# Routing and experts of a two-layer decoder as one block: shared tiles, 40 plain indirect transfers, places mapped expert by expert

## The reference

```python
x = x_btd.reshape(N, Dm)                       # 2048 tokens, already normalised
cap = int(math.ceil(CF * N / E))               # 308 places for each of 8 experts
probs = jax.nn.softmax(x @ Wr + br, axis=-1)
gates, ids = jax.lax.top_k(probs, K)           # K = 2
order = jnp.lexsort((-flat_g, flat_ids))       # by expert, highest gate first
rank = jnp.arange(M) - starts[s_ids]
valid = rank < cap                             # only the 308 highest of an expert are kept
xg = x[disp_tok].reshape(E, cap, Dm)
h = jax.nn.silu(jnp.einsum('ecd,edh->ech', xg, W1) + b1[:, None, :])
out = jnp.einsum('ech,ehd->ecd', h, W2) + b2[:, None, :]
gated = out * disp_g.reshape(E, cap, 1)
y = jnp.zeros((N, Dm), x.dtype).at[disp_tok].add(gated.reshape(E * cap, Dm))
```

## Time and profile before

| | us |
|---|---|
| median of 3 runs | 600.41 (596.93 to 601.2) |
| the profiled execution | 599.32 |
| its span, first to last instruction | 597.2 |
| TensorE busy, share of the span | 469.0, 79% |
| VectorE busy | 332.1, 56% |
| ScalarE busy | 240.4, 40% |
| GpSimd busy | 209.2, 35% |

### The profile page before, as it was taken

The page is one execution under the profiler, slowest core; times in us unless marked ns, Lnnn a source line. Parts: engine busy times, 40 slices in busy tenths (PEclk is TensorE's granted clock), DMA queues, the critical chain, the costliest instruction groups (busy, mean ns, idle before and its releaser), DMA issues. The chain is left out here.

```text
span 597.2 us, 13480 instructions
## 1 busy us (share of the span) xinstructions
PE 469.0 (79%) x5103; PEld 374.5 (63%) x5103; DVE 332.1 (56%) x917; ACT 240.4 (40%) x514; POOL 209.2 (35%) x234
## 2 busy tenths in 40 slices
PE   3899999999986978999999988992663332499950
PEld 1587777777763757899988877781553221266630
DVE  5567677777753535666666652637755667011114
ACT  3766666666552326555555522230220000132313
POOL 3556687799133214000000010316430000557750
PEclk9899999999996999999999987997575555599995
DMA  7970312200000002000000003000024000333317
GB/s 234 386 292 6 143 61 61 63 3 2 4 1 1 0 7 76 1 0 0 0 0 0 0 2 88 19 1 0 1 77 134 1 0 0 103 96 106 113 33 211
DMA packets 31461, 34.72 MB, mean 58 GB/s; under 512 B 5562, under 2 KB 25079, under 8 KB 31289
## 3 DMA queue, kind: packets, MB, share of 16 engines
q1 hardware_dynamic: 29208, 29.50, 15.6%
q0 software_dynamic: 2064, 4.60, 2.4%
q10 hardware_dynamic: 144, 0.00, 0.0%
HBM read 28.65 MB, written 5.46 MB: 57 GB/s over the span
## 5 line engine op out<-in xcount | busy, mean ns | idle before, releaser
L473 DVE TENSOR_REDUCE at_nmax<-bank 128x4 bf16<-128x512 f32 x128 | 82.5, 686 | 44.0 <-PE bank L569 44.0
L413 ACT ACTIVATE at_p<-bank 128x512 f32<-128x512 f32 x128 | 69.2, 596 | 38.2 <-PE bank L588 38.2
L95 POOL TENSOR_TENSOR var<-var,eps 128x12 f32<-128x12 f32 (+1 forms) x8 | 1.6, 206 | 176.4 <-DVE var L88 176.4
L1902 POOL DMA_INDIRECT mo_rows<-mo_n_rows,mo_src_row x24 | 23.0, 959 | 71.3 <-POOLq L1610 64.3
L582 PE MATMUL bank<-ident_b,at_nmax 128*128 128x128 bf16 x512 | 42.8, 221 | 4.3 <-DVE at_nmax L473 3.4
L582 PEld LDWEIGHTS bank<-ident_b,at_nmax 128*128 128x128 bf16 x512 | 30.7, 98 | 18.9 <-issue 9.3
L1975 ACT ACTIVATE mo_h<-bank,mo_b 128x308 f32<-128x308 f32 x32 | 16.5, 517 | 47.5 <-PE bank L1938 47.5
L608 PE MATMUL bank<-at_p,at_v 128*32 128x128 f32 x1024 | 34.7, 276 | 0.9 <-DVE x L490 0.9
L1946 PE MATMUL bank<-mo_w,mo_h 128*128 128x128 f32 (+1 forms) x192 | 33.0, 294 | 1.3 <-ACT mo_h L1975 1.3
L1946 PEld LDWEIGHTS bank<-mo_w,mo_h 128*128 128x128 f32 (+1 forms) x192 | 24.3, 173 | 12.1 <-ACT mo_h L1975 5.3
L1081 PE MATMUL bank<-li_v,li_am 128*128 128x65 f32 x256 | 30.4, 272 | 0.5 <-issue 0.5
(11 more groups left out here) (280 smaller groups left out, 1193.1 us busy)
## 6 DMA issues: line engine op xcount, KB each, us to landing
fo_w<-in_up_stages SPq DMA_DIRECT2D x9, 512.0 KB, 9.3
fo_w<-in_down_stages SPq DMA_DIRECT2D x9, 512.0 KB, 4.7
at_k_ctx<-in_ctx_heads SPq DMA_DIRECT2D x1, 4096.0 KB, 23.9
mo_w<-in_L_ffn_W SPq DMA_DIRECT2D x16, 256.0 KB, 3.1
mo_planes<-ro_zeros POOLq DMA_DIRECT2D x1, 2048.0 KB, 9.1
mo_got<-mo_planes SPq DMA_DIRECT2D x8, 256.0 KB, 5.1
x<-in_x SPq DMA_DIRECT2D x4, 256.0 KB, 3.6
au_ctx<-in_ctx SPq DMA_DIRECT2D x4, 256.0 KB, 3.4
```

The lines of the kernel that those rows point to most:

```text
L413: act.activation(m.p[:, s % 2, J * g:J * g + J, :], bank_t[g][:, :].rearrange("p (j t) -> p j t", j=J), ACT.Exp, scale=scale).then_inc(exp ...
L473: dve.tensor_reduce(m.nmax[:, J * g:J * g + J], bank_s[g % 2][:, :].rearrange("p (j t) -> p j t", j=J), AX.X, ALU.max, negate=True).then_i ...
L1902: pool.indirect_dma_start(out=rows[0:m, e % 2, r, :], out_offset=None, in_=n_rows, in_offset=bass.IndirectOffsetOnAxis(ap=src_row[0:m, til ...
```

## The change

The two blocks become one, `experts` (L1543 of the new kernel), so that engines pass from routing to experts without a common end. Its parts:

- The normalised tokens of all groups stay in one buffer `n` of 136 columns per sequence, 128 features and the 8 values `v`. They are stored as one table after the softmax, rows of 544 bytes, so that a gathered row brings its gates along.
- The softmax and the two highest take 18 operations, some of them interleaved. GpSimd computes which plane an entry goes to (`kind`) while the search begins.
- The search is written out for 10 rounds, with pieces of 6, 6 and 4 sequences.
- Two experts share 5 tiles: two full ones each and one in the middle that holds 52 rows of one expert from row 0 and 52 of the other from row 64. That makes 20 gathers and 20 scatters. Every row of a tile is fetched and stored; unused ones go to spare rows of the planes, so no bounds check is needed.
- Places are mapped expert by expert: `mark` (two comparisons of 1024 columns) and `index` on VectorE, `mapping` (16 matmuls with 6 columns, and one more for the second expert of a pair) on TensorE. Three maps stand before the first transpose, the other five in the loop, each between the second `up` and the first `down`.
- ScalarE copies the transposed rows (`copy_x`) and multiplies the output bias by the gates (`bias`); VectorE's `gate` multiplies the expert's output by the gates and adds that. At the end only two additions per group remain.
- Planes are read back in 4 loads of 512 KB, two from SyncE's and two from ScalarE's queue, and the result is stored from both. Clearing the planes moves from GpSimd's to SyncE's queue. The weights of the first two experts are loaded during the routing.
- The loops over experts are written out.

The core of the diff (indentation shortened):

```diff
-ROWS = [min(128, CAP - r) for r in range(0, CAP, 128)]
-TILES = E6 * len(ROWS)
...
+REST = CAP - 256
+TILES = 5
+SHARED = 2
+ROW = D + E6
+KINDS = 2 + E6
+PIECES = (slice(0, 6), slice(6, 12), slice(12, B))
+FIRST_GATHERS = 2 * TILES
+LATER_GATHERS = (3, 2, 3, 2, 0, 0, 0, 0)
...
-with pe.Fori(0, BITS // ROUND) as i:
-    for b in range(B):
-        if b % HALF == 0:
-            pe.wait_ge(reached_done, 2 * i + b // HALF + 1)
-        mm = pe.matmul(bank_c[:, 0:TRIALS * E6], ones_b[:, :],
-                       reached[:, b, :, :].rearrange("t j e -> t (j e)"),
-                       start=(b == 0), stop=(b == B - 1))
-    mm.then_inc(compared, 1)
...
-for half in range(2):
-    seqs = slice(HALF * half, HALF * half + HALF)
-    dve.tensor_tensor(reached[:, seqs, :, :],
...
-with dve.Fori(0, BITS // ROUND // UNROLL) as i:
-    for k in range(UNROLL):
-        search(UNROLL * i + k)
...
-done(dve.tensor_tensor(at, over(lanes[:, 0:TILES], 2 * B),
-                       hi[:, :, :].rearrange("t k b -> t (k b)").unsqueeze(2)
-                       .to_broadcast([T, 2 * B, TILES]), ALU.is_equal))
...
-dve.wait_ge(lanes_made, 1)
-for k in range(2):
-    dve.tensor_tensor(at_row[:, k, :, :], over(lanes_b[:, :], B),
-                      lo[:, k, :].unsqueeze(2).to_broadcast([T, B, 128]), ALU.is_equal)\
-        .then_inc(rows_marked, 1)
-dve.wait_ge(mapped, 1)
-code, token = code_sum[:, 1, :], code_sum[:, 0, :]
-done(dve.tensor_copy(code_sum[:, :, :], bank_m[:, 0:2 * TILES].rearrange("p (c s) -> p c s", c=2)))
...
-done(dve.tensor_scalar(src_row[:, :], dst_row[:, :], B * T - 1, None, ALU.bitwise_and))
...
-gather(0)
-gather(1)
-for e in range(E6):
-    if e + 2 < E6:
-        pool.wait_ge(turned, e + 1)
-        gather(e + 2)
-    pool.wait_ge(y_added, e + 1)
-    scatter(e)
...
-up(e, par, 0)
-up(e, par, 1)
-down(e, par, 0, first)
-up(e, par, 2)
-down(e, par, 1)
-up(e, par, 3)
-down(e, par, 2)
-if not last:
-    turn(e + 1, 1 - par)
-down(e, par, 3)
...
-for g in range(groups):
-    act.wait_ge(fetched[g], 32)
-    for b in range(Q * g, Q * g + Q):
-        act.activation(got[:, 0, b, :], got[:, 0, b, :], ACT.Copy, scale=gate[0][:, b:b + 1])\
-            .then_inc(gated, 1)
...
-for g in range(groups):
-    dve.wait_ge(fetched[g], 32)
-    for b in range(Q * g, Q * g + Q):
-        dve.scalar_tensor_tensor(out=core.x[:, b, :], in0=got[:, 1, b, :], scalar=gate[1][:, b:b + 1],
-                                 in1=core.x[:, b, :], op0=ALU.mult, op1=ALU.add).then_inc(x_part, 1)
-    seqs = slice(Q * g, Q * g + Q)
-    dve.wait_ge(x_part, Q * (g + 1))
-    dve.wait_ge(gated, Q * (g + 1))
-    dve.tensor_tensor(core.x[:, seqs, :], core.x[:, seqs, :], got[:, 0, seqs, :], ALU.add)\
-        .then_inc(x_done, 1)
...
+def places(e):
+    if e % 2 == 0:
+        return ((0, slice(0, 128), slice(0, 128)), (1, slice(0, 128), slice(128, 256)),
+                (SHARED, slice(0, REST), slice(256, CAP)))
+    return ((SHARED, slice(64, 64 + REST), slice(0, REST)), (3, slice(0, 128), slice(64, 192)),
+            (4, slice(0, 128), slice(192, 320)))
...
+def fetch(eng, g):
+    seqs = slice(Q * g, Q * g + Q)
+    eng.dma_start(got[:, :, seqs, :], by_token[:, 0:2, seqs, :]).then_inc(fetched[g], 16)
...
+sp.wait_ge(levelled, 1)
+sp.dma_start(table[0:B * T, :].rearrange("(t b) c -> t b c", t=T), n[:, :, :]).then_inc(t_out, 16)
+sp.dma_start(table[B * T:B * T + B, :], n[0:B, 0, :]).then_inc(t_out, 16)
...
+def gather(first, last):
+    for at in range(first, last):
+        pair, tile = divmod(at, TILES)
+        pool.wait_ge(indexed, 4 * pair + (3 if tile >= SHARED else 1))
+        pool.indirect_dma_start(
+            out=rows[:, pair, tile, :], out_offset=None, in_=table,
+            in_offset=bass.IndirectOffsetOnAxis(ap=src_row[:, pair, tile:tile + 1], axis=0))\
+            .then_inc(x_in[2 * pair + (tile > SHARED)], 16)
+def scatter(pair, tile):
+    pool.wait_ge(y_done, 6 * pair + (1, 2, 4, 5, 6)[tile])
+    pool.wait_ge(indexed, 4 * pair + (4 if tile >= SHARED else 2))
+    pool.indirect_dma_start(
+        out=planes,
+        out_offset=bass.IndirectOffsetOnAxis(ap=dst_row[:, pair, tile:tile + 1], axis=0),
+        in_=y[:, pair, tile, :], in_offset=None).then_inc(stored, 16)
...
+pool.wait_ge(levelled, 1)
+pool.tensor_tensor(kind[0][:, :], flat(pick[0]), kinds[:, 128:256], ALU.mult).then_inc(kind_step, 1)
...
+gather(0, FIRST_GATHERS)
+at = FIRST_GATHERS
+for e in range(E6):
+    for tile in (range(0, SHARED) if e % 2 == 0 else range(SHARED, TILES)):
+        scatter(e // 2, tile)
+    gather(at, at + LATER_GATHERS[e])
+    at += LATER_GATHERS[e]
...
+    first, count = (0, 3) if e % 2 == 0 else (3, 2)
+    act.activation(xT[:, e // 2 % 2, first * 128:(first + count) * 128], bank_x[:, 0:count * 128],
+                   ACT.Copy).then_inc(x_copied, 1)
+def bias(e):
+    act.wait_ge(x_in[e], 48 if e % 2 == 0 else 32)
+    if e >= 2:
+        act.wait_ge(y_done, 3 * (e - 1))
+    for r, (tile, at, _) in enumerate(places(e)):
+        ins = act.activation(gb2[at, e % 2, r, :], b2[at, e, :], ACT.Copy,
+                             scale=rows[at, e // 2, tile, D + e:D + e + 1])
+    ins.then_inc(biased, 1)
...
+for i in range(ROUNDS):
+    for k, seqs in enumerate(PIECES):
+        pe.wait_ge(reached_done, len(PIECES) * i + k + 1)
+        for b in range(seqs.start, seqs.stop):
+            mm = pe.matmul(bank_c[:, 0:TRIALS * E6], ones_b[:, :],
+                           reached[:, b, :, :].rearrange("t j e -> t (j e)"),
+                           start=(b == 0), stop=(b == B - 1))
+    mm.then_inc(compared, 1)
...
+def mapping(e):
+    pair, odd = divmod(e, 2)
+if odd:
+    pe.wait_ge(indexed, 4 * pair + 2)
+elif pair >= 2:
+    pe.wait_ge(indexed, 4 * (pair - 1))
+for k in range(2):
+    pe.wait_ge(marked, 2 * e + k + 1)
+    for b in range(B // 2 * k, B // 2 * k + B // 2):
+        mm = pe.matmul(bank[:, 4 * odd:4 * odd + 6], at_row[:, e % 2, b, :],
+                       codes[:, :, :, b, e].rearrange("t k c -> t (k c)"),
+                       start=(not odd and b == 0), stop=(b == B - 1), skip_group_check=True)
+if odd:
+    mm = pe.matmul(bank[:, 2 * SHARED:2 * SHARED + 2], core.ident_b[:, :],
+                   spare_b[:, 2 * pair:2 * pair + 2],
+                   start=False, stop=True, skip_group_check=True)
+mm.then_inc(mapped, 1)
...
+for e in range(3):
+    mapping(e)
+turn_x(0)
+for e in range(E6):
+    up(e, 0)
+    up(e, 1)
+    if e + 3 < E6:
+        mapping(e + 3)
+    down(e, 0)
+    up(e, 2)
+    down(e, 1)
+    up(e, 3)
+    down(e, 2)
+    if e + 1 < E6:
+        turn_x(e + 1)
+    down(e, 3)
...
+for seqs in PIECES:
+    count = seqs.stop - seqs.start
+    dve.tensor_tensor(reached[:, seqs, :, :],
...
+def mark(e):
+    if e >= 2:
+        dve.wait_ge(mapped, e - 1)
+    for k in range(2):
+        seqs = slice(B // 2 * k, B // 2 * k + B // 2)
+        dve.tensor_tensor(at_row[:, e % 2, seqs, :], over(lanes_b[:, :], B // 2),
+                          lo[:, seqs, e].unsqueeze(2).to_broadcast([T, B // 2, 128]), ALU.is_equal)\
+            .then_inc(marked, 1)
+dve.wait_ge(mapped, e + 1)
+dve.tensor_copy(low[:, pair, tiles], sums[:, tiles, 1]).then_inc(read_back, 1)
...
+    for dst, seq, per in ((src_row, seq_row, B), (dst_row, low, KINDS * B)):
+        dve.scalar_tensor_tensor(out=dst[:, pair, tiles], in0=sums[:, tiles, 0], scalar=float(per),
+                                 in1=seq[:, pair, tiles], op0=ALU.mult, op1=ALU.add)\
+            .then_inc(indexed, 1)
+def gate(e):
+    dve.wait_ge(down_done, e + 1)
+    dve.wait_ge(biased, e + 1)
+    dve.wait_ge(made, 3)
+    for r, (tile, at, _) in enumerate(places(e)):
+        dve.scalar_tensor_tensor(out=y[at, e // 2, tile, :], in0=y_bank(tile)[at, 0:D],
+                                 scalar=rows[at, e // 2, tile, D + e:D + e + 1],
+                                 in1=gb2[at, e % 2, r, :], op0=ALU.mult, op1=ALU.add)\
+            .then_inc(y_done, 1)
...
+for e in range(4):
+    mark(e)
+    index(e)
+for e in range(E6):
+    if e + 4 < E6:
+        mark(e + 4)
+    gate(e)
+    if e + 4 < E6:
+        index(e + 4)
+for g in range(groups):
+    seqs = slice(Q * g, Q * g + Q)
+    dve.wait_ge(fetched[g], 16)
+    dve.tensor_tensor(core.x[:, seqs, :], core.x[:, seqs, :], got[:, 0, seqs, :], ALU.add)\
+        .then_inc(x_part, 1)
+    dve.wait_ge(x_part, g + 1)
+    dve.tensor_tensor(core.x[:, seqs, :], core.x[:, seqs, :], got[:, 1, seqs, :], ALU.add)\
+        .then_inc(x_done, 1)
```

674 lines of the change are left out of this document (313 added, 361 removed).

## The result

The changed kernel takes 579.62 us, median of 4 runs (579.12 to 579.93). The kernel before took 600.81 in the runs beside it, median of 4 (596.93 to 604.44). The ratio is 0.9656, 95% interval 0.962 to 0.9691. The profiled execution took 579.76, with a span of 578.0, so 1.8 us lie around it.

A forecast was written before the change was run, and what follows sets the result against it. Search bound by VectorE and TensorE taking turns, expert loop by TensorE; 1.3 + 2.0 - 0.8 + 4.0 + 7.6 - 2.0 + 0.3 + 1.9 = 14.3 off 599.32 gave 585.0 us, range 580 to 592.

The forecast's parts named there:

- Scores: Start of the stage: two TensorE waits go, late tokens' variance costs 0.8; gain 1.3 us (0 to 2.2).
- Top two: After the scores: 18 VectorE instructions for 22, 5.0 us for 7.05; gain 2.0 us (1 to 3).
- search: Ten search rounds of 2.46 us for 2.81: gain 4.0 (2 to 5), less 0.8 for GpSimd's kinds beside the first.
- Flags to the first transposes: Between search and experts: shorter mapping before the gathers, 18.0 us for 25.6; gain 7.6 (4 to 9).
- second rival: Marks and gathers delay each other in the first map's chain, or the tail gives nothing: 587 to 594 us, chance 0.22.
- Tail: Reading back and adding planes: 13.5 us for 15.4, first loads arriving at 5.0; gain 1.9 (0 to 4).
- Cost of the loop 2.0 (0 to 5.5): Expert loop: five maps and wider odd experts, less a last wait for rows, make it 2.0 us longer.
- The step of 7.07 us ... stays TensorE's: Expert loop: TensorE still sets the step, its length of 7.07 us unchanged apart from added work.
- 5 x 0.4: Expert loop: five maps between second up and first down cost 0.4 us each, 2.0 in all (0 to 4).
- 0.4 for the 320 columns: Expert loop: odd experts multiply 320 columns for 308, 4% of 4 x 2.6 us, costing 0.4.
- fourth rival: More gain comes: maps within TensorE's gaps and a tail at full transfer speed, 580 us (577 to 582), chance 0.12.
- first rival: Expert loop: GpSimd's queue of forty transfers becomes the bound, slower than before; 608.5 us at pitch 2.4, chance 0.04.

The follow-up runs named there:

- cleared gathers: Changed kernel with the third and fourth expert's marks held back until the first three gathers landed: 580.37 us alone, 578.6 us together with two other edits.

## Why the prediction was right, and where it failed

The direction held, and the mechanism in every stretch but the expert loop. **Scores:** the two waits were 2.7; the variance cost 0.69 (442.48 to 443.17 in the timeline) and left one wait of 0.59. I had taken off 0.6 for gaps that did not come. **Top two** and **search** came within 0.4: 2.34 for 2.0, and 3.0 for 4.0 - 0.8, with rounds of 2.49 for 2.46 and 0.66 for the kinds, shown by putting them off. **Flags to the first transposes:** 17.13 for 18.0. The index was done at 13.58 for 13.9 (added up exactly, the prediction's own terms give 13.6), and the third gather followed it after 0.39 and not 0.77, and a gather that is not held up lands after some 2.5, not 3.35; with the 0.6 that the mark took from it, it was 3.1. The second rival's mechanism was there, for 0.6 on the third gather and up to 0.4 on the first instead of its 3.0, and it hit GpSimd: the marks of the changed kernel were not slowed. One of the prediction's signs of being wrong, gathers above 1.5 us, came four times (1.55, 1.90, 1.74 and 1.74); only the first of these stood on the path, and no transpose within the loop waited for rows. **Tail:** 13.45 for 13.5, in part by luck: the first group came 4.66 after the issue for 5.0, and VectorE then waited 0.50 for the third group, which the sum had not.

**The step that failed** is the expert loop, "Cost of the loop 2.0 (0 to 5.5)": it gained 1.86. With that alone put right the sum gives 581.1, within the stated range. Three parts of it:
- "The step of 7.07 us ... stays TensorE's", with the same length, was wrong. The partial tile cost 0.28 in each step and the registers 0.09. The first showed in the trace of before, as a gap of 0.17 without a releaser in the weight loads, which I had not opened; the second was half of the wait of 0.19 for ScalarE, which I had taken as room for the maps. The last step's wait of 0.4, which I had counted, and this shorter step together gave 1.0 there.
- "5 x 0.4" for the maps: 0.15 to 0.25 each in the four steps that can be compared, 0.8 in all. The first step cannot be compared, since its clock differs.
- 0.4 for the 320 columns: an odd expert's step without a map is 0.22 longer than an even one's, but 0.16 of that is the third transpose in its turn, which leaves 0.06.

The bound "0 to 5.5" had no favourable side, although a step that gets another tile shape and another loop can fall as well as rise. That put the fourth rival (580, from 577 to 582) at 0.12, where the result lies. Half of that rival's reason held, the maps within TensorE's gaps; the other half, a tail at full speed, did not. The first rival asked whether GpSimd would become the bound. It nearly was the bound before, and in the changed kernel TensorE no longer waits for it. The prediction set the pitch of 1.26 against the steps of the new kernel alone; against the old one, six transfers are 7.56 for a step of 7.07.

## What to carry to other kernels

Count an engine's queue and not its busy time: transfers that are 0.96 us busy stood 1.28 apart, so 73% busy was a full queue, and a faster TensorE gained nothing. When a change replaces a loop's partial tiles, open the weight loads and look for gaps without a releaser before you put the step down as unchanged; when it writes a loop out, ask how much of a wait stood there for the registers. Judge edits of less than 1 us by the length of their own stretch in the trace: search, mapping and each step from the second expert on repeated to 0.1 us from run to run, while the runs of one kernel spread over up to 8. The tail repeated only to 0.7.

## What the runs showed that I had not expected

- The first expert's step took 8.32, 8.47, 8.52, 9.55, 10.47, 10.70 and 10.71 us in runs that differ in none of TensorE's instructions there, and 8.80 and 12.58 in the two with cleared gathers, by when the granted clock rose from 0.50 (1.2 GHz) to 1.00 (2.4 GHz) while TensorE was busy nearly all the time (13.42 of 14.0 us in the longest). The rise came 5.1 us after the first transposes in the run of 8.32, where the mean clock of the step was 0.78, and 13.9 after them in that of 12.58, where it was 0.51. What is won just ahead of such a rise may come back as time at the lower clock.
- The stage began between 438.29 and 446.92 us in runs of the changed kernel and its variants, with the same code ahead of it; the page's clock row shows lower slices at other places in these runs. What decides that, I did not test.
- A 52-row weight tile costs TensorE 0.17 us of gap at the change of shape, and 0.28 in the step with what follows.
- A gather that meets a running VectorE instruction with two SBUF inputs ended 0.81 to 0.86 us after that instruction in six cases of seven; the one that started together with it was not delayed.
